# Second routed experts: a 32 bit product as three products of rounded halves

## The chip, the cores and the metric

One Trainium2 chip, one NeuronCore. The metric is the time of one execution on the device in microseconds (us); less is better. The engines named here are PE (TensorE; PEld is its weight load), DVE (VectorE), ACT (ScalarE), POOL (GpSimd) and SP (SyncE).

## The reference

Sixteen sequences of 256 rows of 128 features (4096 rows) go through four sublayers, each added to its input and normalised: attention with 16 heads of 64, routed experts (8, two for each row, F = 512), attention with 16 heads of 8, and a second block of experts. The change lies in the last one:

```python
sh = gelu(jnp.einsum('nd,sdh->snh', xf, sw1) + sb1[:, None, :])          # S = 2 shared experts, all rows
shared_out = (jnp.einsum('snh,shd->nd', sh, sw2) + sb2.sum(0)) / S
topv, topi = jax.lax.top_k(xf @ router_w + router_b, TOP_K)              # 2 of E = 8
h = gelu(jnp.einsum('nd,edh->enh', xf, w1) + b1[:, None, :])             # D = 128, H = 256
y = jnp.einsum('enh,ehd->end', h, w2) + b2[:, None, :]
moe_out = jnp.einsum('ne,end->nd', comb, y)                              # only the chosen ones count
```

## The kernel before

The program is a row of stages. `attention0_routed0` and `attention1` scatter each row, once for each of its two experts, into a table in HBM (`xs`), ordered by expert. `routed1` then takes the table in N = 39 blocks of BR = 256 rows, all of one block for one expert. `final1` gathers, weighs and normalises the results. A block ends each stage: an engine that is through with its list waits there for the others.

For block j `routed1` does this:

- SP loads the block's rows (`xrow`, 8 slots).
- PE turns them (`turn_input`, two 128x128 transposes, L1284) into XT, one PSUM bank that serves every block in turn.
- ACT copies XT to `x` (`turned`, L1354, two slots) and counts `x_done`. PE's next `turn_input` waits for that count.
- DVE copies the expert's first weights to `wu` (`weights`, L1395, four slots), works out the rows' destinations (`destinations`, L1409) and counts `w_done`.
- PE multiplies (`up`, L1266: two products of 128x128 weights with 256 columns in float32, each of which is two records in the trace).
- ACT applies gelu (`units`, L1347).
- PE multiplies with the second weights (`down`, L1276), DVE adds the bias and moves the result to `yrow` (`output`, L1401), and POOL scatters it to HBM with two indirect DMAs (L1254). `yrow` has eight slots.

Between these lie the shared experts for the last LATE = 3 groups of 512 rows, in KS = 12 steps, one for every three blocks: `shared_up` (PE, L101 to L103, three products of 512 columns), `shared_hidden` (ACT, gelu L1366 and a rounded copy L1369), `shared_low` (DVE, L1419), `shared_down` (PE, L101 to L103), and after four such steps `shared_rows` (PE, L1309) and `add_shared` (DVE, L1425). Also ACT makes two diagonals for each of the first 32 blocks (L1360). When PE is through with the last `down` it does `residual` for eight banks (L1313) and is then at the end of the stage.

The order of work on each engine is written out by hand: engines run their own lists in order, and only semaphores tie them together. The orders around the change are these loops over j:

```python
# PE                                  # ACT                             # DVE
up(j); down(j - 1)                    units(j)                          weights(j + 2); destinations(j)
turn_input(j + 2)                     shared_hidden((j - 2) / 3)        output(j - 1)
shared_up((j - 1) / 3)                turned(j + 2)                     shared_low((j - 2) / 3)
shared_down((j - 3) / 3)              diagonals(j)
```

where a shared step stands only at the j that is divisible. Elsewhere in the kernel (`attention0_routed0`, and the shared steps here) a product is already made of halves by `split_mm`: a high half is the value rounded to float32r, the low half is the rest, and three products are summed: high times high, low times high, high times low.

Of the kernel before, what the change touches and what calls it, by code (L numbers as in the profile page):

```python
# [12 lines left out]
F32 = mybir.dt.float32  # L13
F32R = mybir.dt.float32r
# [3 lines left out]
ALU = mybir.AluOpType  # L18
# [3 lines left out]
P = 128  # L22
# [1160 lines left out]
def routed1(nc, ctx, g, d):  # L1183
# [5 lines left out]

    expert, w_at, in_at = g.expert, g.w_at, g.in_at  # L1190
    xrow = sb("xrow", [P, XSLOTS, 2, XW])
    wu = sb("wu", [P, WSLOTS, F1])
    dest = sb("dest", [P, YSLOTS, 2], U32)
    x = sb("x", [P, 2, BR])
    hid = sb("hid", [P, 2, FB1, BR])
    yrow = sb("yrow", [P, YSLOTS, 2, P])
    th, pr = sb("th", [P, NTL]), sb("pr", [P, 2, NTL])
# [10 lines left out]
    def shared_step(j, at):  # L1208
        k = (j - at) // 3
        return k if (j - at) % 3 == 0 and 0 <= k < KS else None  # L1210
# [5 lines left out]
    xt_ps, x_done, up_ps, act_done, down_ps, y_done, dest_done = (sem(n) for n in (  # L1216
        "xt_ps", "x_done", "up_ps", "act_done", "down_ps", "y_done", "dest_done"))
    x_in = [sem(f"x_in{k}") for k in range(XSLOTS)]
    w_done = sem("w_done")
    y_out = [sem(f"y_out{k}") for k in range(YSLOTS)]  # L1220
    may_scatter, th_done, pr_done = sem("may_scatter"), sem("th_done"), sem("pr_done")

    def after(eng, signal, n):

        if n > 0:
            eng.wait_ge(signal, n)
# [6 lines left out]
    with nc.Block(no_gpsimd_drain=True) as block:  # L1233
# [26 lines left out]
        def _(pe):  # L1260
            def up(j):
                pe.wait_ge(x_done, j + 1)
                after(pe, act_done, j - 1)
                pe.wait_ge(w_done, j + 1)
                for f in range(FB1):
                    last = nc.tensor.matmul(H[:, j % 2, f * BR:(f + 1) * BR], wu[:, j % WSLOTS, f * P:(f + 1) * P], x[:, j % 2, :],  # L1266
                                            start=True, stop=True)
                last.then_inc(up_ps, 1)

            def down(j):  # L1270
# [69 lines left out]
        @block.scalar  # L1340
        def _(act):
            def units(j):
                w = offset(mybir.EngineType.Activation, j)
                act.wait_ge(up_ps, j + 1)
                after(act, down_ps, j - 1)
                for f in range(FB1):
                    last = nc.scalar.activation(hid[:, j % 2, f, :], H[:, j % 2, f * BR:(f + 1) * BR], ACT.Gelu,  # L1347
                                                bias=g.w1[:, bass.ds(w + (W1C + f), 1)])
                last.then_inc(act_done, 1)

            def turned(j):
                act.wait_ge(xt_ps, j + 1)
                after(act, up_ps, j - 1)
                nc.scalar.activation(x[:, j % 2, :], XT, ACT.Copy).then_inc(x_done, 1)  # L1354

            def diagonals(k):
                if k == 0:
                    act.wait_ge(pr_done, 2)
                for c in range(2):
                    nc.scalar.activation(g.diag[:, k, c, :], g.ident[:], ACT.Copy, scale=pr[:, c, k:k + 1])  # L1360

            def shared_hidden(k):
                w = k % W
                act.wait_ge(sup_ps, k + 1)
                after(act, shid_done, k - W + 1)
                nc.scalar.activation(shid[:, w, :], UP[:, k % 2, :], ACT.Gelu, bias=g.b1[:, w:w + 1]).then_inc(sact_done, 1)  # L1366
                act.wait_ge(sact_done, k + 1)
                after(act, sdown_ps, k - W + 1)
                nc.scalar.activation(shid_h[:, w, :], shid[:, w, :], ACT.Copy).then_inc(shi_done, 1)  # L1369

            def shared_mean(m):
                act.wait_ge(sdown_ps, m * W + W)
                after(act, ser_ps, m - 1)
                nc.scalar.activation(syt[:, m % 2, :], YE, ACT.Identity, bias=g.sb2m[:, 1:2], scale=1.0 / S1
                                     ).then_inc(sye_done, 1)

            nc.scalar.activation(th[:], g.gap[:], ACT.Tanh, scale=0.5).then_inc(th_done, 1)
            for j in range(-2, N):
                if 0 <= j:
                    units(j)  # L1380
                if shared_step(j, 2) is not None:
                    shared_hidden(shared_step(j, 2))
                if j + 2 < N:
                    turned(j + 2)
                if shared_group(j, 3 * W + 1) is not None:
                    shared_mean(shared_group(j, 3 * W + 1))
                if 0 <= j < NTL:
                    diagonals(j)

        @block.vector  # L1390
        def _(dve):
            def weights(j):
                w = offset(mybir.EngineType.DVE, j)
                after(dve, up_ps, j - WSLOTS + 1)
                nc.vector.tensor_copy(wu[:, j % WSLOTS, :], g.w1[:, bass.ds(w, F1)]).then_inc(w_done, 1)  # L1395

            def output(j):
                w = offset(mybir.EngineType.DVE, j)
# [27 lines left out]

            weights(0)
            weights(1)
            for j in range(N + 1):
                if j + 2 < N:  # L1430
                    weights(j + 2)
                if j < N:
                    destinations(j)
                if 0 <= j - 1:
                    output(j - 1)
                if shared_step(j, 2) is not None:
                    shared_low(shared_step(j, 2))
                if shared_group(j, 3 * W + 3) is not None:
                    add_shared(shared_group(j, 3 * W + 3))
# [1467 lines left out]
```

## Time and profile before

| what | value |
|---|---|
| three runs | 1343.93, 1343.99, 1346.85 us (median 1343.99) |
| the profiled execution | 1343.33 us |
| its span in the trace | 1341.5 us |
| mean granted clock of TensorE | 0.978 of full speed |
| busy share of the span | PE 93%, PEld 80%, DVE 73%, ACT 69%, POOL 46% |
| where `routed1` lies in the span | about 1202.5 to 1314.3 us |

The span runs from the first instruction to the last. A busy share is an average over stages with different limits; what one stage is worth is read from its own rows. Times in rows are microseconds from the span's start. A record of PE is drawn from where it starts to where its modelled end is, so records overlap, and the pace is read from start to start.

### The profile page before, as it was taken

The numbers are of one execution on the slowest core, as the hardware profiler recorded it, in microseconds if no ns is written. First come the engines' busy times: TensorE is split into PE (matmuls) and PEld (weight loads), VectorE is DVE, ScalarE is ACT, GpSimd is POOL, SyncE is SP. The second block draws the span as 40 slices with busy tenths as digits, with TensorE's granted clock in tenths as the row PEclk, the third lists the DMA queues.
The fourth block names the chain that finished last, engine by engine and source line by source line (L and its number), as shares of the span: only waits on it lengthen the run. The fifth ranks groups of instructions, "written<-read, shape, count | busy, mean of one in ns | idle before, by whom it ended". The sixth has DMA issues, their size and how long they took to land. (4 is left out here: it accounts for less than half of the span.)

```text
span 1341.5 us, 34497 instructions
## 1 busy us (share of the span) xinstructions
PE 1252.5 (93%) x10783; PEld 1070.9 (80%) x10784; DVE 976.9 (73%) x2973; ACT 921.5 (69%) x2434; POOL 618.2 (46%) x967
## 2 busy tenths in 40 slices
PE   6999999999999999999999489999999998869996
PEld 5888888888888887899999367777777776658985
DVE  6777788788878888766666488898989887363443
ACT  4777777777777776656665367878778786758863
POOL 3244444444444443453343524556556552336773
PEclk9999999999999999999999679999999999999998
DMA  8012212121202021021111522022115101113326
GB/s 267 21 53 69 67 52 75 45 85 35 91 28 92 28 88 58 15 71 57 56 54 38 190 92 77 22 89 86 43 65 174 49 17 45 60 33 106 110 73 198
DMA packets 56445, 99.82 MB, mean 74 GB/s; under 512 B 11184, under 2 KB 46384, under 8 KB 53744
## 3 DMA queue, kind: packets, MB, share of 16 engines
q1 hardware_dynamic: 45840, 78.58, 18.5%
q0 software_dynamic: 9088, 18.89, 4.2%
q10 hardware_dynamic: 1440, 1.39, 0.3%
q8 instruction: 40, 0.66, 0.2%
q14 instruction: 37, 0.30, 0.1%
HBM read 77.85 MB, written 62.06 MB: 104 GB/s over the span
## 5 line engine op out<-in xcount | busy, mean ns | idle before, releaser
L326 ACT ACTIVATE a_prob<-psum,a_nmx 128x128 f32<-128x128 f32 (+1 forms) x512 | 208.3, 425 | 82.4 <-DVE a_nmx L631 82.4
L530 POOL TENSOR_TENSOR a_prob<-a_prob,a_rl 128x128 f32<-128x128 f32 (+1 forms) x256 | 124.3, 508 | 244.1 <-DVE a_rl L635 243.5
L2373 DVE TENSOR_REDUCE a_nmx<-psum 128x2 f32<-128x512 f32 x256 | 170.1, 685 | 22.0 <-PE psum L1658 19.2
L333 ACT ACTIVATE a_probt<-psum 128x768 f32<-128x768 f32 x128 | 105.1, 821 | 70.8 <-PE psum L961 70.8
L2030 ACT ACTIVATE a_prob<-psum 128x1024 f32<-128x1024 f32 x128 | 127.3, 1024 | 7.5 <-PE psum L1688 7.3
L1658 PE MATMUL psum<-k_stk,a_q_stk 96*128 96x256 f32 x512 | 116.1, 320 | 12.8 <-DVE a_nmx L2373 8.6
L577 POOL DMA_INDIRECT yt<-a_yrow,a_dest x78 | 75.2, 964 | 101.3 <-ACT a_yrow L373 87.1
L1658 PEld LDWEIGHTS psum<-k_stk,a_q_stk 96*128 96x128 f32 x512 | 78.3, 194 | 43.3 <-issue 18.3
L326 ACT ACTIVATION_READ_ACCUMULATOR a_prob<-psum,a_nmx 128x1 f32 x512 | 107.8, 211 | 0.0
L961 PE MATMUL psum<-ident,a_prob 128*128 128x128 f32 x768 | 106.1, 274 | 1.4 <-DVE a_prob L641 1.0
L620 DVE TENSOR_TENSOR a_qkt<-psum,a_bqk 128x512 f32<-128x512 f32 x128 | 88.2, 689 | 21.7 <-PE psum L103 21.3
L773 DVE TENSOR_TENSOR a_hid<-a_wv,psum 128x512 f32<-128x512 f32 x78 | 53.6, 688 | 60.3 <-PE psum L103 44.5
L101 PE MATMUL psum<-a_x_h,a_wqk_h 128*128 128x256 f32 x312 | 94.3, 302 | 2.3 <-DVE a_wqk_l L779 2.1
L1254 POOL DMA_INDIRECT yt<-m_yrow,m_dest x78 | 75.5, 968 | 41.5 <-issue 21.2
L101 PE MATMUL psum<-a_xt_h,a_wqk_h 128*128 128x256 f32 x256 | 81.9, 320 | 8.0 <-DVE a_xt_l L616 6.9
L103 PE MATMUL psum<-a_x_l,a_wqk_h 128*128 128x256 f32 x312 | 88.1, 283 | 0.0
L102 PE MATMUL psum<-a_x_h,a_wqk_l 128*128 128x256 f32 x312 | 88.1, 282 | 0.0
L961 PEld LDWEIGHTS psum<-ident,a_prob 128*128 128x128 f32 x768 | 85.8, 141 | 2.1 <-POOL a_prob L530 1.0
L631 DVE TENSOR_REDUCE a_nmx<-psum 128x2 f32<-128x512 f32 x128 | 87.1, 680 | 0.0
L1688 PE MATMUL psum<-a_q_stk,k_stk 128*128 128x256 f32 x512 | 85.4, 290 | 0.2 <-DVE a_o L2388 0.2
L2229 POOL DMA_INDIRECT xs<-a_nrm,a_idx x60 | 61.6, 1027 | 43.3 <-DVE a_idx L2459 24.9
L2015 ACT ACTIVATE k_stk<-psum,a_in_head 96x256 fp32r<-96x256 f32 x192 | 74.5, 467 | 9.8 <-PE psum L1652 9.7
(385 smaller groups left out, 3859.6 us busy)
## 6 DMA issues: line engine op xcount, KB each, us to landing
xs<-in_fill SPq DMA_DIRECT2D x144, 264.0 KB, 4.3
a_xrow<-xs SPq DMA_DIRECT2D x39, 132.0 KB, 2.1
m_xrow<-xs SPq DMA_DIRECT2D x39, 132.0 KB, 2.2
w<-in_w SPq DMA_DIRECT2D x16, 256.0 KB, 3.5
a_yin<-yt SPq DMA_DIRECT2D x16, 256.0 KB, 2.6
f_yin<-yt SPq DMA_DIRECT2D x7, 512.0 KB, 8.2
w<-in_wr SPq DMA_DIRECT2D x2, 1284.0 KB, 7.7
xs<-in_fill_idle SPq DMA_DIRECT2D x2, 1056.0 KB, 6.6
```

The lines of the kernel that those rows point to most:

```text
L101: nc.tensor.matmul(out, wh, xh, start=start, stop=False)
L102: nc.tensor.matmul(out, wl, xh, start=False, stop=False)
L103: return nc.tensor.matmul(out, wh, xl, start=False, stop=stop)
L326: last = nc.scalar.activation(prob[:, hp % 4, h, at], S[:, 2 * (hp % 2) + h, at], ACT.Exp, bias=nmx[:, hp % 4, q, h:h + 1], accum_out=lsum ...
L333: nc.scalar.activation(probt[:, hp % 2], PT[:, :, 0:SW], ACT.Copy).then_inc(pt_done, 1)
L530: last = nc.gpsimd.tensor_tensor(prob[:, hp % 4, 0, at], prob[:, hp % 4, 0, at], rl[:, hp % 4, 0, q:q + 1].to_broadcast(prob[:, hp % 4, 0, ...
L620: nc.vector.tensor_tensor(qkt[:, hp % 2], QK.rearrange("p (j t) -> p j t", j=2), bqk[:, hp, :].unsqueeze(2).to_broadcast([P, 2, T]), ALU.a ...
L631: nc.vector.reduce_max(nmx[:, hp % 4, 1, :], two[:, :, P:SW], AX.X, negate=True).then_inc(nmx_done, 1)
L961: last = nc.tensor.transpose(PT[:, h, k * P:(k + 1) * P], prob[:, hp % 4, h, k * P:(k + 1) * P], g.ident[:])
L1658: last = nc.tensor.matmul(bank[:, q * T:(q + 1) * T], q_stk[0:KR, p, h // HG, q * P:(q + 1) * P], k_stk[p][0:KR, h, :], start=True, stop=True)
L2030: nc.scalar.activation(prob[:, k % 2, 2 * (t % 2):2 * (t % 2) + 2, :], ST[:, 2 * (t % 2):2 * (t % 2) + 2, :], ACT.Exp, scale=SCALE).then_i ...
L2373: nc.vector.reduce_max(nmx[:, :, h:h + 1], bank.rearrange("p (q k) -> p q k", q=QB), AX.X, negate=True).then_inc(mx_done, 1)
```

## The change

The two float32 products of `up` become six of halves through `split_mm`. ACT's copy of XT is now a rounding to `x_h`, DVE's copy of the weights a rounding to `wu_h`. DVE gets two new instructions for each block: `weights_low` (`wu_l`, SBUF minus SBUF, 128x256) and `input_low` (`x_l`, XT in PSUM minus `x_h`, 128x256). The counts `w_done` and `x_done` now come from these two, and new counts (`wh_done`, `xh_done`) tie them to the high halves. XT is therefore free for the next `turn_input` only when `input_low` has read it. In DVE's list both stand behind `output(j - 1)` and ahead of `shared_low`.

```diff
-    wu = sb("wu", [P, WSLOTS, F1])
+    wu_h, wu_l = sb("wu_h", [P, WSLOTS, F1], F32R), sb("wu_l", [P, WSLOTS, F1], F32R)
-    x = sb("x", [P, 2, BR])
+    x_h, x_l = sb("x_h", [P, 2, BR], F32R), sb("x_l", [P, 2, BR], F32R)
...
                 for f in range(FB1):
-                    last = nc.tensor.matmul(H[:, j % 2, f * BR:(f + 1) * BR], wu[:, j % WSLOTS, f * P:(f + 1) * P], x[:, j % 2, :],
-                                            start=True, stop=True)
+                    units = slice(f * P, (f + 1) * P)
+                    last = split_mm(nc, H[:, j % 2, f * BR:(f + 1) * BR], wu_h[:, j % WSLOTS, units], wu_l[:, j % WSLOTS, units],
+                                    x_h[:, j % 2, :], x_l[:, j % 2, :], True, True)
...
-                nc.scalar.activation(x[:, j % 2, :], XT, ACT.Copy).then_inc(x_done, 1)
+                nc.scalar.activation(x_h[:, j % 2, :], XT, ACT.Copy).then_inc(xh_done, 1)
...
-                nc.vector.tensor_copy(wu[:, j % WSLOTS, :], g.w1[:, bass.ds(w, F1)]).then_inc(w_done, 1)
+                nc.vector.tensor_copy(wu_h[:, j % WSLOTS, :], g.w1[:, bass.ds(w, F1)]).then_inc(wh_done, 1)
+
+            def weights_low(j):
+                w = offset(mybir.EngineType.DVE, j)
+                dve.wait_ge(wh_done, j + 1)
+                nc.vector.tensor_tensor(wu_l[:, j % WSLOTS, :], g.w1[:, bass.ds(w, F1)], wu_h[:, j % WSLOTS, :].bitcast(F32), ALU.subtract
+                                        ).then_inc(w_done, 1)
+
+            def input_low(j):
+                dve.wait_ge(xh_done, j + 1)
+                after(dve, up_ps, j - 1)
+                nc.vector.tensor_tensor(x_l[:, j % 2, :], XT, x_h[:, j % 2, :].bitcast(F32), ALU.subtract).then_inc(x_done, 1)
...
             weights(0)
             weights(1)
+            weights_low(0)
+            weights_low(1)
+            input_low(0)
+            input_low(1)
             for j in range(N + 1):
...
                     output(j - 1)
+                if j + 2 < N:
+                    weights_low(j + 2)
+                    input_low(j + 2)
                 if shared_step(j, 2) is not None:
                     shared_low(shared_step(j, 2))
```

## Rows read from the trace of the kernel before

**Rows 1.** The chain that ended last, in order of time: start, us, what

```profile
1315.30 6.06 DMA f_yin<-yt
...
1321.40 12.79 PE psum L2716 x112
```

**Rows 2.** Busy us of each engine in one stretch, PEclk, DMA share, GB/s

```profile
1250.00:1260.00 10.00, 10.00 (x66) 8.95 (x65) 3.94 (x13) 8.07 (x23) 7.56 (x9) 1.00 0.37 106
```

**Rows 3.** Timeline of POOL alone, 1200 to 1341: start, us, instruction, idle before

```profile
1213.37 0.95 POOL L1254 DMA_INDIRECT yt<-m_yrow,m_dest  x1 [17.88 <-DVE m_yrow L1401]
...
1216.01 0.96 POOL L1254 DMA_INDIRECT yt<-m_yrow,m_dest  x1 [0.42 <-issue]
...
1311.55 0.95 POOL L1254 DMA_INDIRECT yt<-m_yrow,m_dest  x1 [0.31 <-DMA yt<-m_yrow,m_dest]
```

**Rows 4.** Line 1233, the stage's end: ns min/median/max, first and last start

```profile
L1233 PEldq EVENT_SEMAPHORE  x2: 51/51/51, 1313.5 to 1314.3; - x2
...
L1233 POOLq COMPARE_BRANCH  x1: 38/38/38, 1314.0 to 1314.0; - x1
```

**Rows 5.** Timeline of all engines from 1305: PE's last work in the stage

```profile
1306.35 7.03 PE L1313 MATMUL psum<-x,ident 128*128 128x512 f32 x16
```

**Rows 6.** Timeline of all engines, 1250 to 1257, around one shared step

```profile
1250.50 1.03 PE L1266 MATMUL psum<-m_x,m_wu 128*128 128x256 f32 x4
...
1252.39 0.69 ACT L1366 ACTIVATE m_shid<-psum,b 128x512 f32<-128x512 f32 x1
...
1253.11 0.63 ACT L1369 ACTIVATE k_stk<-m_shid 128x512 fp32r<-128x512 f32 x1
...
1253.65 0.37 ACT L1354 ACTIVATE m_x<-psum 128x256 f32<-128x256 f32 x1
1253.78 0.69 DVE L1419 TENSOR_TENSOR k_stk<-m_shid,k_stk 128x512 fp32r<-128x512 f32 x1 [0.78 <-ACT k_stk L1369]
...
1254.52 0.51 PE L101 MATMUL psum<-k_stk,ws 128*128 128x512 f32 x1
...
1255.33 1.03 PE L1266 MATMUL psum<-m_x,m_wu 128*128 128x256 f32 x4
```

**Rows 7.** Timeline of PE alone, the rest of that period

```profile
1256.19 1.05 PE L1276 MATMUL psum<-w,m_hid 128*128 x8
...
1258.00 0.38 PE L1266 MATMUL psum<-m_x,m_wu 128*128 128x256 f32 x1
```

**Rows 8.** Timeline of all engines in the first routed experts, 560 to 566

```profile
560.85 0.36 PE L101 MATMUL psum<-a_x_h,a_wqk_h 128*128 128x256 f32 x1
...
561.04 0.28 PE L102 MATMUL psum<-a_x_h,a_wqk_l 128*128 128x256 f32 x1
...
562.24 0.28 PE L103 MATMUL psum<-a_x_l,a_wqk_h 128*128 128x256 f32 x1
...
562.78 0.39 ACT L378 ACTIVATE a_x_h<-psum 128x256 fp32r<-128x256 f32 x1 [0.34 <-PE psum L1037]
...
563.22 0.42 DVE L784 TENSOR_TENSOR a_x_l<-psum,a_x_h 128x256 fp32r<-128x256 f32 x1
...
563.55 0.21 DVE L786 SCALAR_TENSOR_TENSOR a_dest<-a_xrow,t_expert 128x2 uint32<-128x2 f32 x1
```

**Rows 9.** Timeline of DVE alone, two stretches (outputs of blocks 2 and 35)

```profile
1216.65 0.41 DVE L1395 COPY m_wu<-w 128x256 f32 x1
...
1217.12 0.42 DVE L1401 TENSOR_TENSOR m_yrow<-psum,w 128x256 f32<-128x256 f32 x1
1217.59 0.29 DVE L1395 COPY m_wu<-w 128x256 f32 x1
...
1300.27 0.42 DVE L1401 TENSOR_TENSOR m_yrow<-psum,w 128x256 f32<-128x256 f32 x1 [0.16 <-issue]
```

**Rows 10.** Timeline of all engines, 1200 to 1216: the first block's product

```profile
1206.87 1.91 PE L1266 MATMUL psum<-m_x,m_wu 128*128 128x256 f32 x4
```

**Rows 11.** Busy us and PEclk ahead of the first scatter, as in rows 2

```profile
1210.00:1212.00 2.00, 2.00 (x14) 1.82 (x12) 0.00 (x0) 1.46 (x5) 0.00 (x0) 0.72 0.60 175
```

More of the change, by code:

```diff
@@ L1218, in routed1 @@
     x_in = [sem(f"x_in{k}") for k in range(XSLOTS)]
-    w_done = sem("w_done")
+    w_done, wh_done, xh_done = sem("w_done"), sem("wh_done"), sem("xh_done")
     y_out = [sem(f"y_out{k}") for k in range(YSLOTS)]
```

## Prediction

> **What bounds the kernel now.** I read four views, from the end backwards. The chain that ended last says only that the last stage is bound by a DMA and then by PE [rows 1]; that stage starts when `routed1` ends and is not touched, so the question is when `routed1` ends. The windows come next: in the middle of the stage PE counts as busy for all of 10 us, ACT for 8.07, POOL for 7.56, DVE for 3.94 [rows 2]. That points at PE, and a faster product on PE would then pay at once.
>
> POOL's own timeline says otherwise. Its 78 scatters of one block after another start from 1213.37 to 1311.55 [rows 3], which is 98.18/77 = 1.275 us from start to start, for 0.95 us of work and about 0.3 us of issue, almost never with a wait for data. A block costs POOL 2.55 us and three blocks 7.65. POOL is the reader's first suspect: a bound that its 46% of the span hides. The stage's end confirms it. PE reaches it at 1313.5, POOL at 1314.0 [rows 4], so POOL decides, and PE with the 16 residual records behind its last `down` [rows 5] is only 0.5 us ahead.
>
> PE's pace has to be read from start to start. An `up` starts at 1250.50 and the same one of the next shared step at 1258.00 [rows 6, 7]: 7.50 us for three blocks. PE and POOL run almost level. And PE isn't simply full: in each period there is a closed loop through ACT and DVE that sets the 7.50. It reads [rows 6, 7]: `up` start to the gelu of `shared_hidden` 1.89 (1250.50 to 1252.39); to its rounded copy 0.72; to `shared_low` 0.67; to `shared_down` 0.74; to the next `up` 0.81; that `up` 0.86; then `down`, transposes and `shared_up` to the next period's `up` 1.81. The sum is 7.50. `shared_down` starts 0.05 us after `shared_low` ended (1253.78 + 0.69 = 1254.47) [rows 6], so DVE's subtraction is what PE waits for there.
>
> **PE's products.** Two float32 products take 0.86 us (1255.33 to 1256.19) [rows 6, 7]. Products of halves with the same 256 columns stand in the first routed experts: twelve in a row, the second starts 0.19 us after the first, which follows float32 work, and then ten steps take 1.20 us, 0.12 each [rows 8]. Six cost 0.72 us behind other products of halves, and 0.79 behind float32 transposes. A period has two `up` of the first kind (behind `shared_up` and `shared_down`) and one of the second: PE gives back 0.14 + 0.14 + 0.07 = 0.35 us in three blocks, 4.4 us in 38. Since POOL sets the end, by itself this would buy almost nothing.
>
> What the pages say goes one step further: the Trainium skill (FP8 and Floating Point Precision, TensorE Precision Notes) has true float32 as four passes of the array. Three passes for four would make `up` 0.645 us instead of 0.72; the loop below would come to 7.71, and the time to about 1345.4. The row at 0.12 us per product stands against it, and I stay with the row.
>
> **DVE's new work.** `input_low` has its twin in the first routed experts: it starts 0.44 us after ACT's rounding started (562.78 to 563.22) and lets the next instruction go 0.33 us later [rows 8]. `weights_low` has no twin of its size with both inputs in SBUF; between the 0.42 of that PSUM form and the 0.69 of the 512 wide `shared_low` [rows 6, 8] I take 0.42, it being half as wide. Together 0.84 us per block, 3.3 us in the 10 us window, on top of 3.94 [rows 2]: DVE goes to about 7.3 of 10 and is not full. `weights_low` is hidden: it runs behind `output`, while ACT is still on its shared work. Without this cover it would cost 0.34 to 0.42 in each shared step. The 39 copies of `weights` (0.29 each, 0.41 where one was held up [rows 9]) stay; if the rounding makes all of them 0.41, the 0.12 lies in DVE's idle time too. ACT's rounding costs what its copy cost, 0.37 against 0.39 [rows 6, 8]. SP's and POOL's lists don't change.
>
> **The new wait.** `input_low` is not hidden in a shared step. ACT does the gelu and the rounded copy of `shared_hidden` before `turned`, and DVE's list has `input_low` ahead of `shared_low`. Before, `shared_low` started 0.67 after the copy L1369. Now ACT first starts `turned` (0.54 after L1369 [rows 6]), DVE waits 0.44 for it, and `shared_low` goes 0.33 later: 1.31 in place of 0.67. Behind `shared_low` stand the next `weights`, `destinations` and `output`; PE waits with `shared_down` and all behind it, POOL for that output. `turn_input` also waits for `input_low`, but for 0.4 us that lie inside the same wait.
>
> The loop becomes (1.89 - 0.14) + 0.72 + 0.54 + 0.44 + 0.33 + 0.74 + 0.81 + 0.72 + 1.81 = 7.86 us. That is over POOL's 7.65: the loop takes over as the bound, and the products that got faster bring nothing.
>
> **The sum.** From the output of block 2 (1217.12) to that of block 35 (1300.27) there are 11 periods, 83.15 us [rows 9]: 82.5 by the loop, and 0.65 where `shared_rows` comes in and PE has no slack. With the wait there is slack, so I count 11 x 7.86 = 86.46, which is +3.3. Behind the last period's start comes one more wait, 0.64 less the 0.14 of the `up` ahead of it, and the last two `up` give back 0.14 + 0.07: +0.3. So PE reaches the end of the stage at 1313.5 + 3.6 = 1317.1. POOL: block 35's output is at 1300.27 + 3.3 + 0.5 = 1304.1, done at 1304.5, and four blocks of 2.55 take POOL to 1314.7; it was through at 1312.5 and at the end at 1314.0, so now it is there at 1316.2. PE is later. The stage ends 1317.1 - 1314.0 = 3.1 us later, and the last stage follows unchanged.
>
> The start I take at nothing, between two bounds. At the low clock (0.72 on average from 1210 to 1212, so it rises near 1211.1 [rows 11]) the first `up` took 1.91 [rows 10]; six products at twice 0.12 would take about 1.4, and the first `input_low` adds 0.44 ahead of the second `turn_input`. The ends are -0.5 and +0.5.
>
> The profiled execution took 1343.33 us, of which the span is 1341.5; plus 3.1 it would be 1346.4. The median of the runs is 1343.99, and plus 3.1 it is 1347.1, my forecast. That is 0.23%, inside the 0.3% (4.0 us: 1339.96 to 1348.02) below which a measurement of this kernel doesn't tell a change from none. Its own range is 1345.5 to 1348.7: the start's 0.5 and 0.1 us in each of the 11 periods, either way.
>
> **Rivals.** *POOL stays the bound.* If the loop grows to 7.65 or less, because the wait is shorter by 0.2 us a step than I put together from other places, POOL's 78 scatters set the end as before: 1343.7 to 1344.5. For it speaks that POOL and PE are now level, against it the closed sum of the loop, which fits the old period to 0.01. Chance 0.20.
>
> *The clock rises later.* PE now waits more in the first blocks, and before the rise it did nothing at high clock since 1206.87 [rows 10]. If the rise came later by as long as PE had worked at the low clock then, 4.2 us, it would lose half of them, 2.1 us: 1349.2, slower. Against it: PE is still busy most of that time. Chance 0.12.
>
> *Issue on DVE.* `weights_low` reads its offset from SBUF ahead of the instruction. If each new instruction kept the next waiting 0.1 us more, the loop would be 8.06 and the time 1347.1 + 2.2 = 1349.3. Chance 0.10.
>
> *POOL is slowed.* A copy of 0.41 in place of 0.29 lay beside the scatter of 1216.01 [rows 3, 9], so the two engines can meet, and here the scatter kept its 0.96. If `weights_low` lengthened every scatter by that 0.12, POOL would need 78 x 1.395 = 108.8 us from 1213.37, end at 1322.2 and be at the stage's end at 1323.7: 9.7 us slower, 1353.7. It decides from 0.04 us per scatter (3 us over 78). The Trainium skill (SBUF — State Buffer, Who interferes with whom) has a two-port copy on VectorE holding up the descriptor writing of POOL's DMAs, and a subtraction with both inputs in SBUF contending only with POOL's reads. By that rule the new subtractions would leave the scatters alone; the trace shows the meeting but not POOL's loss. Chance 0.06.
>
> *Faster by over 4 us* would need POOL's pace below 1.22 us, under every step in its timeline: 0.03.
>
> **How the numbers follow.** My forecast holds 0.49, of which 0.07 is above 1348.02. Slower is 0.07 + 0.12 + 0.10 + 0.06 = 0.35, within 0.3% 0.42 + 0.20 = 0.62, faster 0.03. The range reaches down into the case of POOL (1343.6) and up over the two cases near 1349 (1349.8); what is left out is POOL slowed, faster, and the outer parts of the others.
>
> **What would show it.** Right: `shared_low` starts about 1.3 us after L1369, PE waits for DVE ahead of `shared_down` about 0.8 us each time, the period is near 7.86, POOL waits for `output` once a period, and PE is the last to reach line 1233. Wrong: POOL without waits and a period of 7.65; or scatters above 1.275 from start to start while their outputs are long ready; or PEclk at 0.5 after 1212.

## The result and the profile after

| | before | after |
|---|---|---|
| median of the runs on the same chips | 1343.85 us (22 runs) | 1347.36 us (22 runs) |
| ratio, 95% interval | | 1.0027 [1.0021, 1.0034] |
| the profiled execution, its span | 1343.33, 1341.5 us | 1348.51, 1346.7 us |
| `routed1`, from SP's first load of rows to the stage's end | 1202.97 to 1314.35: 111.4 us | 1203.80 to 1317.29: 113.5 us |
| the last stage, from there to the end of the span | 27.15 us | 29.4 us |

The forecast was 1347.1 us. The change costs 3.5 us, and the quicker products of `up` bring nothing to the end. In the profiled pair the difference is 5.2 us: `routed1` starts 0.8 later, takes 2.1 longer, and the last stage takes 2.2 longer. The 0.8 comes from unchanged code: over all 14 profiles of this study `routed1` starts between 1202.46 and 1204.82, with the old products as with the new. The way from the first load to the output of block 2 varies too, from 13.3 to 14.8 us, with the old products (13.3 to 14.2) as with the new: the granted clock rises 6.2 us after the first load in one profile and 9.2 in another. The length of a stage in one profile is therefore good to about a microsecond. What repeats is the way from the output of block 2 to that of block 35: 83.1 and 83.2 us in the two profiles with the old products and lists (`before`, `warm_before`), 85.7 in all three of the changed ones (`after`, `after_again`, `warm_after`).

Timeline of all engines in the changed kernel, 1250 to 1260, around one shared step (as in [rows 6]); the columns are start, length, instruction and what it waited for:

```profile
1252.33 0.28 PE L101 MATMUL psum<-m_x_h,m_wu_h 128*128 128x256 f32 x1
1252.33 0.42 DVE L1401 TENSOR_TENSOR m_wu_l<-w,m_wu_h 128x256 fp32r<-128x256 f32 x1 [0.17 <-issue]
...
1253.04 1.05 PE L1277 MATMUL psum<-w,m_hid 128*128 x8
...
1254.07 0.69 ACT L1367 ACTIVATE m_shid<-psum,b 128x512 f32<-128x512 f32 x1
...
1254.79 0.63 ACT L1370 ACTIVATE k_stk<-m_shid 128x512 fp32r<-128x512 f32 x1
...
1255.33 0.36 ACT L1355 ACTIVATE m_x_h<-psum 128x256 fp32r<-128x256 f32 x1
...
1255.73 0.43 DVE L1407 TENSOR_TENSOR m_x_l<-psum,m_x_h 128x256 fp32r<-128x256 f32 x1 [0.46 <-ACT m_x_h L1355]
1256.07 0.68 DVE L1431 TENSOR_TENSOR k_stk<-m_shid,k_stk 128x512 fp32r<-128x512 f32 x1
...
1256.30 0.41 PE L1285 MATMUL psum<-ident,m_xrow 128*128 128x128 f32 x2 [0.23 <-DVE m_x_l L1407]
1256.67 0.29 DVE L1396 CAST m_wu_h<-w 128x256 fp32r x1
1256.74 1.05 POOL L1254 DMA_INDIRECT yt<-m_yrow,m_dest  x1 [0.30 <-issue]
1256.80 0.19 PEld L101 LDWEIGHTS psum<-k_stk,ws 128*128 128x128 f32 x1 [0.33 <-DVE k_stk L1431]
1256.81 0.50 PE L101 MATMUL psum<-k_stk,ws 128*128 128x512 f32 x1
...
1257.62 0.28 PE L101 MATMUL psum<-m_x_h,m_wu_h 128*128 128x256 f32 x1
...
1258.22 0.96 POOL L1254 DMA_INDIRECT yt<-m_yrow,m_dest  x1 [0.43 <-issue]
1258.32 1.05 PE L1277 MATMUL psum<-w,m_hid 128*128 x8
```

The same of PE alone, 1251 to 1262, the next period's `up`:

```profile
1260.12 0.28 PE L101 MATMUL psum<-m_x_h,m_wu_h 128*128 128x256 f32 x1
```

Read it from `up` at 1252.33, as [rows 6] were read: to the gelu 1.74, to the rounded copy 0.72, to `turned` 0.54, to `input_low` 0.40, to `shared_low` 0.34, to `shared_down` 0.74, to `up` 0.81, that `up` 0.70, and 1.80 to the next `up` at 1260.12. The sum is 7.79 us; the prediction had put 7.86 together from other places. DVE waits 0.46 for ACT's `turned`, and PE waits 0.23 ahead of the transposes and 0.33 ahead of `shared_down`.

Line 1233, the stage's end, in the changed kernel (as [rows 4]):

```profile
L1233 PEldq EVENT_SEMAPHORE  x2: 51/51/51, 1317.0 to 1317.2; - x2
...
L1233 POOLq COMPARE_BRANCH  x1: 38/38/38, 1316.2 to 1316.2; - x1
```

PE is now the last, at 1317.0, and POOL comes at 1316.2. The order has turned round.

The first and the last scatter on POOL's timeline in the changed kernel (as [rows 3]):

```profile
1213.93 1.02 POOL L1254 DMA_INDIRECT yt<-m_yrow,m_dest  x1 [17.63 <-DVE m_yrow L1413]
...
1313.77 0.96 POOL L1254 DMA_INDIRECT yt<-m_yrow,m_dest  x1 [0.30 <-DMA yt<-m_yrow,m_dest]
```

That is 99.84/77 = 1.297 us from start to start, against 1.275. Twelve times, once in a period, POOL is idle for 0.43 in place of 0.30, as at 1258.22 above: it waits for the output. The long scatters add about as much as before (1.0 us, 0.8 before).

One stretch of the stage in the changed kernel, columns as in [rows 2]:

```profile
1250.00:1260.00 10.00, 9.68 (x73) 8.83 (x73) 6.91 (x22) 7.58 (x22) 7.31 (x8) 1.00 0.37 109
```

DVE went from 3.94 to 6.91 (7.3 foreseen). PE is no longer busy all the time, which is the trace of the new wait. DVE's new instructions last 0.42 us each (35 of each kind in the middle of the stage: mean 0.425 and 0.420), as foreseen.

The chain that ended last, in the changed kernel (as [rows 1]):

```profile
1317.29 4.62 DMA f_yin<-yt
...
1321.95 17.39 PE psum L2735 x128
```

And the windows of the last stage, in the changed kernel:

```profile
1319.00:1321.00 2.00, 0.00 (x0) 0.00 (x0) 0.00 (x0) 0.00 (x0) 0.00 (x0) 1.00 0.88 271
1321.00:1323.00 2.00, 1.05 (x5) 1.06 (x6) 0.00 (x0) 0.00 (x0) 0.00 (x0) 0.52 0.70 217
1323.00:1325.00 2.00, 2.00 (x11) 2.00 (x11) 0.00 (x0) 0.00 (x0) 0.00 (x0) 0.50 1.03 341
1325.00:1327.00 2.00, 2.00 (x11) 2.00 (x11) 1.19 (x9) 0.00 (x0) 0.00 (x0) 0.50 1.09 385
1327.00:1329.00 2.00, 2.00 (x16) 2.00 (x15) 0.60 (x5) 0.00 (x0) 1.04 (x1) 0.78 1.09 386
```

Before the change, the same view has two such stretches:

```profile
1317.00:1319.00 2.00, 1.90 (x9) 1.90 (x10) 0.00 (x0) 0.00 (x0) 0.00 (x0) 0.50 0.81 244
1319.00:1321.00 2.00, 1.68 (x9) 1.49 (x8) 0.28 (x2) 0.00 (x0) 0.00 (x0) 0.66 0.94 299
```

PE waited for the first load for 5.0 us (3.7 before), and when it began, at 1321.95, the granted clock was at the lower of its two levels, 1.2 GHz (0.50): from 1321.07 to 1327.90, 6.8 us in place of 3.4. Before, that low stretch was spent on 16 products ahead of a second load, which PE had to wait for anyway (the chain of [rows 1] is a load of 6.06 us and then 112 products). After, the chain is the first load and all 128 products, many of them at half speed.

### The profile page after: what moved, and what is told of

Its sections match the earlier page's. It is cut to its first block and busy times, and to the rows that moved or that the text cites. A ratio compares the mean times of both kernels' runs of the same rounds, so it can differ in the third digit from the quotient of the medians.

```text
span 1346.7 us, 34846 instructions
## 1 busy us (share of the span) xinstructions
PE 1253.0 (93%) x10861; PEld 1072.5 (80%) x10862; DVE 1002.4 (74%) x3051; ACT 923.1 (69%) x2434; POOL 618.8 (46%) x967
## 5 line engine op out<-in xcount | busy, mean ns | idle before, releaser
L1677 PE MATMUL psum<-k_stk,a_q_stk 96*128 96x256 f32 x512 | 116.2, 320 | 12.6 <-DVE a_nmx L2392 8.4
```

Source lines behind the costliest of these rows:

```text
L1677: last = nc.tensor.matmul(bank[:, q * T:(q + 1) * T], q_stk[0:KR, p, h // HG, q * P:(q + 1) * P], k_stk[p][0:KR, h, :], start=True, stop=True)
```

## The experiments

Twelve runs, each beside runs of the kernel before on the same chip. The median of those was 1342.86 us beside `wait_only`, `no_input_low` and the two `down_later`, 1343.65 beside `reordered` and the `warm` runs, and 1344.13 beside `no_weights_low`, `no_lows`, `turned_first` and `after_again`. So compare ratios, and not medians, across the table. "Stage" is `routed1` and "last" the last stage, in the profiled execution, measured as in the first table. The two columns on POOL split its time from the first to the last scatter: idle time over the usual 0.30 ahead of a scatter, and length over the usual 0.96 of scatters that are longer.

| run | median us | ratio [95%] | stage | last | POOL idle, long |
|---|---|---|---|---|---|
| before | 1343.85 | 1 | 111.4 | 27.15 | 0.1, 0.8 |
| the change | 1347.36 | 1.0027 [1.0021, 1.0034] | 113.5 | 29.4 | 1.5, 1.0 |
| `after_again` | 1348.34 | 1.0025 [1.0015, 1.0035] | 112.9 | 28.9 | 1.5, 0.9 |
| `wait_only` | 1349.46 | 1.0047 [1.0033, 1.0060] | 117.1 | 26.3 | 5.4, 1.0 |
| `no_weights_low` | 1347.94 | 1.0035 [1.0022, 1.0048] | 113.2 | 29.3 | 1.9, 0.9 |
| `no_input_low` | 1345.74 | 1.0024 [1.0015, 1.0033] | 112.0 | 28.0 | 0, 2.0 |
| `no_lows` | 1346.99 | 1.0017 [1.0008, 1.0025] | 112.2 | 28.7 | 0, 1.8 |
| `reordered` | 1347.22 | 1.0027 [1.0018, 1.0036] | 113.0 | 27.6 | 0, 3.0 |
| `turned_first` | 1347.29 | 1.0022 [1.0013, 1.0030] | 113.1 | 28.2 | 1.5, 0.5 |
| `down_later_after` | 1349.34 | 1.0044 [1.0031, 1.0058] | 116.2 | 28.3 | 3.4, 1.2 |
| `down_later_before` | 1346.93 | 1.0026 [1.0015, 1.0036] | 113.5 | 29.5 | 3.0, 0.1 |
| `warm_before` | 1343.31 | 0.9999 [0.9990, 1.0008] | 110.5 | 26.7 | 0.1, 0.8 |
| `warm_after` | 1346.26 | 1.0024 [1.0015, 1.0033] | 113.0 | 27.2 | 1.5, 1.0 |
| `warm_reordered` | 1346.54 | 1.0022 [1.0013, 1.0032] | 113.6 | 27.05 | 0, 2.9 |

Without these two parts POOL's way from first to last scatter is a constant: 98.18 - 0.12 - 0.79 = 97.3 us before, and 97.2 to 97.5 in the change, `reordered`, `no_lows`, `no_input_low` and `wait_only`.

All versions but `warm_before` are slower than the kernel before by an interval that leaves out 1. Among themselves most can't be told apart: of the versions with the new products only `down_later_after` lies above the change by nearly a whole interval, and taking the wait away (`no_input_low`, `no_lows`, `reordered`) gives back nothing that the medians resolve. What separates them are the rows of their profiles, one execution each: these show what sets the stage's end.

**Is it the wait for `input_low`?** Three runs take the change apart. The first adds the wait and nothing else to the kernel before:

```diff
-                nc.scalar.activation(x[:, j % 2, :], XT, ACT.Copy).then_inc(x_done, 1)
+                nc.scalar.activation(x[:, j % 2, :], XT, ACT.Copy).then_inc(xh_done, 1)
...
+            def input_low(j):
+                dve.wait_ge(xh_done, j + 1)
+                after(dve, up_ps, j - 1)
+                nc.vector.tensor_tensor(x_l[:, j % 2, :], XT, x[:, j % 2, :], ALU.subtract).then_inc(x_done, 1)
```

> The kernel before with its float32 products, plus input_low on DVE in its place, whose result nobody reads, and with x_done counted by it. Theory: the loop grows by 0.64 to 8.14 us, 11 periods give 7.0 less the 0.65 of slack, plus 0.6 in the last one: 7 us, 1351. The wait costs more than the change lost, because the faster products had hidden part. Rival, that the two subtractions are hidden on DVE: 1344.

Its timeline of all engines, around a shared step:

```profile
1256.42 0.63 ACT L1369 ACTIVATE k_stk<-m_shid 128x512 fp32r<-128x512 f32 x1
1256.96 0.36 ACT L1354 ACTIVATE m_x<-psum 128x256 f32<-128x256 f32 x1
...
1257.36 0.42 DVE L1400 TENSOR_TENSOR m_x_l<-psum,m_x 128x256 fp32r<-128x256 f32 x1 [1.06 <-ACT m_x L1354]
1257.70 0.68 DVE L1424 TENSOR_TENSOR k_stk<-m_shid,k_stk 128x512 fp32r<-128x512 f32 x1
...
1258.43 0.19 PEld L101 LDWEIGHTS psum<-k_stk,ws 128*128 128x128 f32 x1 [0.33 <-DVE k_stk L1424]
```

From L1369 to `shared_low` it is 1.28 us, as in the changed kernel (1254.79 to 1256.07), against 0.67 before. With the old, slower products the period is 8.09 (from the `shared_low` at 1249.61 to that at 1257.70), 0.59 above 7.50, and the stage is 5.7 us longer: 11 x 0.59 less the 0.65 of slack. The wait does that by itself, in the median too (1.0047), and the new products then take back 3.6 us of it in the profiled stages. It is near what was expected of it (a loop of 8.14, and 7 us).

The other two leave out one of the low halves each. In `no_weights_low` the third product reads `wu_h` where `wu_l` stood, and the subtraction is gone:

```diff
-            weights_low(0)
-            weights_low(1)
...
-                    weights_low(j + 2)
```

> The changed kernel without weights_low: the second product takes wu_h in place of wu_l (the low half of the weights is left out). input_low stays where it was. Theory of the loop: weights_low was hidden, so the period stays at 7.79 us and the time at 1347, within 1 us. Rival, that the sum of DVE's new work sets the pace: half of the loss comes back, 1345.5.

The period is 7.79, the same as in the changed kernel, and so are PE's waits (0.22 and 0.34). So `weights_low` is hidden, as the prediction had it. The median, 1347.94, is where it was expected.

`no_input_low` does the same with `input_low`, and ACT's rounding counts `x_done` again:

```diff
-                nc.scalar.activation(x_h[:, j % 2, :], XT, ACT.Copy).then_inc(xh_done, 1)
+                nc.scalar.activation(x_h[:, j % 2, :], XT, ACT.Copy).then_inc(x_done, 1)
...
-                    input_low(j + 2)
```

> The changed kernel without input_low: the third product takes x_h in place of x_l (the low half of the rows is left out) and ACT counts x_done. weights_low stays. Theory: the loop is 7.50 - 0.28 = 7.22 us, under POOL's 7.65, so POOL sets the end: 1344. Rival, that weights_low, or six products in place of two, or DVE's load is the loss: 1347.

Line 1233 in `no_input_low`:

```profile
L1233 PEldq EVENT_SEMAPHORE  x2: 51/51/51, 1308.5 to 1314.5; - x2
...
L1233 POOLq COMPARE_BRANCH  x1: 38/38/38, 1314.2 to 1314.2; - x1
```

PE is through 5.7 us ahead of POOL, so the wait is gone and POOL decides again. But the kernel isn't back at 1.000, as I had expected: POOL waits for nothing and needs 1.2 us more than before, all of it in longer scatters, of up to 1.40 us. That and the 0.85 us of its last stage are not all of the 3 us that its ratio of 1.0024 stands for; the rest stays open. `no_lows` leaves out both low halves:

> The changed kernel without both subtractions: the second and third products take the high halves again (all low halves are left out), ACT and DVE's rounding count x_done and w_done. Six products remain. Theory that DVE's subtractions lengthen some of POOL's scatters (1.302 us from start to start in reordered, 1.291 in no_input_low, 1.275 before): here POOL is back at 1.275, its 78 scatters take 98.2 us from first to last start, and PE waits 5 us or more at the stage's end. Time 1343 to 1345, the last stage's low clock included. Rival, that six products or the rounding copy slow POOL: 1.29 or more, and 1345.5 or more.

There too PE is far ahead (1310.5, POOL 1316.1), the loop is 7.19, and POOL still loses 1.0 us more in long scatters than before. Its pace is 1.289 us from start to start. So the theory that DVE's new subtractions lengthen the scatters failed here: both are gone, and the scatters are still longer. What lengthens them comes below.

**Can the wait be had for nothing?** Two orders of work that keep all of it. `reordered` puts DVE's `input_low` behind `shared_low`, and PE's `shared_down` ahead of `turn_input` in the shared steps:

```diff
-                if j + 2 < N:
+                if j + 2 < N and shared_step(j, 3) is None:
...
+                    if j + 2 < N:
+                        turn_input(j + 2)
...
-                    input_low(j + 2)
                 if shared_step(j, 2) is not None:
                     shared_low(shared_step(j, 2))
+                if j + 2 < N:
+                    input_low(j + 2)
```

> The changed kernel, all its work kept, with two swaps: DVE does shared_low ahead of input_low, and PE does shared_down ahead of turn_input in a shared step. Theory of the closed loop: shared_low starts 0.67 after the rounded copy again, and what waits for input_low is now behind shared_down, so the loop is 7.50 - 2 x 0.14 = 7.2 us, under POOL's 7.65. POOL sets the stage's end as in no_input_low, PE reaches it some 5 us earlier than POOL. The last stage may then start with PE at its low clock, as there: 1345.5; without that effect 1343. Rival, that two more DVE instructions or six products cost in themselves: 1347.

PE is 4.1 us ahead of POOL (1311.7 and 1315.8), and POOL never waits. Still the time is that of the change, 1347.22, where 1343 to 1345.5 was expected: the 1.4 us of waiting that POOL no longer has came back as 2.0 us in longer scatters (pace 1.302).

`turned_first` moves ACT's `turned` ahead of `shared_hidden`:

```diff
-                if shared_step(j, 2) is not None:
-                    shared_hidden(shared_step(j, 2))
                 if j + 2 < N:
                     turned(j + 2)
+                if shared_step(j, 2) is not None:
+                    shared_hidden(shared_step(j, 2))
```

> The changed kernel, all its work kept, with ACT doing turned(j + 2) ahead of shared_hidden. DVE's wait for ACT's rounding goes, but the gelu now stands behind turned, which waits for PE's transposes: from the end of up(j) 0.89 + 0.22 + 0.31 = 1.42 to turned, 0.26 to the gelu, 0.72, 0.67, 0.74 to shared_down: 3.81 us, against 0.31 + 0.72 + 0.72 + 0.54 + 0.44 + 0.33 + 0.74 = 3.80 now. Theory of the loop: no gain, 1347 within 1 us. Rival, that the queue behind input_low on DVE is the cause by itself: it goes, and 2 us come back, 1345.

PE no longer waits for `input_low`, but it waits for `shared_low` for 5.0 us in all (12 times, up to 0.5). The loop goes through `turned` all the same, now ahead of the gelu, and the period is 7.73.

Two runs move PE's `shared_down`, and `shared_mean`, `shared_rows` and `add_shared` with it, one block later, once in the changed kernel and once in the one before:

```diff
-                if shared_step(j, 3) is not None:
-                    shared_down(shared_step(j, 3))
+                if shared_step(j, 4) is not None:
+                    shared_down(shared_step(j, 4))
```

> The changed kernel with shared_down (and the mean, rows and add behind it) one block later in the lists. Theory of the closed loop through input_low: PE no longer stands behind shared_low, a period is PE's own sum, 2 x 0.72 + 0.79 + 3 x (0.89 + 0.22) + 2 x 0.78 = 7.1 us, which is under POOL's 7.65, so POOL sets the end again: about 1344 us, level with the kernel before. Rival, that the loss comes from DVE's load on POOL or from the last stage: it stays near 1347.

> The kernel before with the same move. Theory: PE's wait for shared_low goes too, but POOL's 78 scatters set the end, so nothing changes: 1344, within 1 us; PE's outputs come earlier and wait for POOL. Rival, that PE's pace of 7.50 was the bound: PE's own sum is 3 x (0.86 + 0.89 + 0.22) + 2 x 0.78 = 7.47, which would also change little; the two differ in whether POOL waits for output, which by the theory it never does.

I had expected 1344 of the first and no change of the second, and both are slower. PE's waits in `down_later_after` over the middle of the stage (who waited for what: total, times, longest):

```profile
PE psum L1277 <- DVE m_yrow L1413: 3.5, 11, 0.8
PE psum L1285 <- DVE m_x_l L1407: 2.8, 12, 0.3
```

The wait for `shared_low` is gone and two others are there: `turn_input` waits for `input_low`, since XT is a single bank, and `down` waits for the output of the block before. The period is 7.97 in place of 7.79. So the 0.4 us of `turn_input`, which the prediction took to lie inside the wait for `shared_low`, are a wait of their own once that one is removed. The move also costs something by itself, as the kernel before shows. It puts `shared_down` right behind `shared_up` in one block, so one output in three comes late. DVE's outputs and POOL's scatter there, in `down_later_before`:

```profile
1251.04 0.42 DVE L1401 TENSOR_TENSOR m_yrow<-psum,w 128x256 f32<-128x256 f32 x1 [1.87 <-PE psum L1276]
...
1254.06 0.42 DVE L1401 TENSOR_TENSOR m_yrow<-psum,w 128x256 f32<-128x256 f32 x1 [1.61 <-PE psum L1276]
...
1255.27 0.96 POOL L1254 DMA_INDIRECT yt<-m_yrow,m_dest  x1 [0.80 <-DVE m_yrow L1401]
```

The two outputs are 3.02 us apart where POOL needs one every 2.5, and POOL waits 3.0 us in all. The theory had it that POOL never waits.

**What lengthens the scatters.** In `no_lows`, the timeline of all engines around one of them:

```profile
1251.81 0.96 POOL L1254 DMA_INDIRECT yt<-m_yrow,m_dest  x1 [0.30 <-issue]
...
1253.01 0.69 DVE L1431 TENSOR_TENSOR k_stk<-m_shid,k_stk 128x512 fp32r<-128x512 f32 x1 [0.79 <-ACT k_stk L1370]
1253.07 1.47 POOL L1254 DMA_INDIRECT yt<-m_yrow,m_dest  x1 [0.30 <-issue]
```

And in `reordered`:

```profile
1254.77 0.42 DVE L1403 TENSOR_TENSOR m_wu_l<-w,m_wu_h 128x256 fp32r<-128x256 f32 x1
1254.82 1.20 POOL L1254 DMA_INDIRECT yt<-m_yrow,m_dest  x1 [0.30 <-DVE m_yrow L1415]
```

Each time the scatter starts while DVE is already inside an instruction that reads SBUF alone, and ends 0.83 or 0.84 after that instruction has ended: 1253.70 to 1254.54 and 1255.19 to 1256.02. In the changed kernel's first fence the scatter at 1256.74 stands 0.07 inside the cast that ends at 1256.96, and ends at 1257.79. I took all 14 profiles together. `shared_low`, `weights_low` and the copy or cast of `weights` read SBUF alone. Of the scatters that start at least 0.06 us inside one of them with at least 0.17 left, all 107 end 0.82 to 0.85 after it (18, 17 and 72 for the three). Of the 46 or so that start within 0.03 of its start, inside it or just ahead, none is longer than 0.96; there the DVE instruction is up to 0.05 longer instead. `input_low`, `output` and `add_shared` read PSUM, and `destinations` is 0.21 long; of some 110 scatters that start as far inside one of these four, none is longer than 0.97. No long scatter stands outside this pattern. So DVE can hold a scatter that starts late by what is left of its instruction, less 0.13. That is read from rows, not tried: no run moved one of these instructions to free a scatter.

Between 0.03 and 0.06 both occur (the scatter at 1254.82 is 0.05 inside). This says where the gain went in `reordered`: its 13 long scatters are four that start inside `shared_low`, eight inside `weights_low` and one inside the cast, while the changed kernel has twelve short holds by the cast alone. In `no_lows` all five scatters that are longer than 1.00 are held by `shared_low`, an instruction of the kernel before: its 1.8 us need no new instruction, only that the scatters start at other moments of DVE's work.

The Trainium skill (SBUF — State Buffer, Who interferes with whom) says that a DVE instruction in a mode with two ports, which a copy can enter, and an instruction of GpSimd exclude each other: whoever is first has the shared port pair for the whole instruction. It says too that a subtraction with both inputs in SBUF contends only with an instruction of GpSimd that reads SBUF. Where the copy is first the rows agree with the first, to the 0.06 us that decides who was first. Where the scatter is first it holds the copy only in a part of its time. Of 56 copies that start 0.52 to 0.72 us into a scatter, 53 end 1.05 after the scatter's start, so that they take up to 0.53 in place of 0.29 (as the 0.41 in [rows 9]); the 187 that start earlier, or after 0.76, take 0.32 at the most. From the second the prediction concluded that the new subtractions leave the scatters alone, and that does not hold: 17 scatters were held by `weights_low` and 18 by `shared_low`. A scatter takes its row numbers from `m_dest` in SBUF, so it may be one of the instructions that read; no run here tells.

**The last stage.** In the `warm` runs PE has work for a part of its wait at the boundary: the last `residual` is written out as a product of its own, and three products of the same kind stand ahead of the first of the last stage, where PE would be idle (`warm_reordered` also does that `residual` six times more at the end of `routed1`):

```diff
+            for _ in range(2):
+                nc.tensor.matmul(g.psum[:, NG - 1, :], g.ident[:], g.x1[:, (NG - 1) * GT:NG * GT], start=True, stop=True)
+            nc.tensor.matmul(g.psum[:, NG - 1, :], g.ident[:], g.x1[:, (NG - 1) * GT:NG * GT], start=True, stop=False)
```

> The kernel before, with PE kept busy between the stages: residual of bank 7 is done twice more, to no effect on the result, and its real one stands at the head of the last stage (2.6 us of PE work in a gap of 3.7). Theory of the clock in the last stage: PE's granted clock doesn't fall there, the first group's 16 products take 1.8 us in place of 3.6; they are waited for by DVE, but the second group's data come only at 1321.4, so little is gained: 0 to 1.5 us faster, 1341.5 to 1343. Rival, that the clock there costs nothing: the same.

> The changed kernel with the same extra work on PE. In its profile the clock was low from 1321.2 to 1328.0 and the last stage took 29.4 us against 27.2. Theory: if that is part of what the change lost, it comes back: 1 to 2.5 us less than the changed kernel, about 1345. Rival, that the loss is all in the wait in the stage: 1347.

> reordered with PE kept busy to the end of the stage (bank 7's residual six times more) and into the last one, as in warm_after. Theory: no wait in the loop and no low clock: as warm_before, 1341.5 to 1343. Rival: as reordered.

The chain of `warm_after` and one of its windows:

```profile
1317.82 6.08 DMA f_yin<-yt
...
1323.94 12.79 PE psum L2735 x112
```

```profile
1321.00:1323.00 2.00, 1.69 (x15) 1.69 (x16) 0.00 (x0) 0.00 (x0) 0.00 (x0) 1.00 0.69 229
```

The clock stays at its higher level (1.00), and the chain has the form of [rows 1] again: 16 products are done ahead of the second load, and 112 behind it take 12.79 us. The last stage is 27.2 us, against 29.4 and 28.9. The first load is as late here (4.5 us from issue to landing) as in the changed kernel, so the late load by itself is not what cost the time; the low clock behind it was. In the kernel before the low clock costs nothing that can be measured: `warm_before` is at 0.9999 [0.9990, 1.0008].

The other profiles add two things. The length of the low stretch doesn't follow from that of PE's idle time: it is 6.8 us after 4.4 to 5.0 us of idle PE in four profiles (both of the changed kernel, `no_weights_low`, `down_later_after`), but 3.4 after 5.0 in `turned_first`, and 10.2 after 3.3 in `down_later_before`. And the late load costs the more, the longer PE then runs at the low clock: the last stage takes 27.2 us without a low stretch (`warm_after`), 28.2 with 3.4 us of it (`turned_first`), and 28.9 and 29.4 with 6.8 (the changed kernel). With an early load 3.4 us of it do no harm (26.3 in `wait_only`), but the 10.2 us in `down_later_before` make 29.5. What sets the length of the low stretch stays open.

In the medians little of this is seen. Those of the warm pair are 2.95 us apart (1.0024 and 0.9999), those of the two kernels of this case 3.5 (1.0027). The difference, 0.55 us, is what the low clock would cost the change in a median, by this estimate; it lies inside the intervals, so it isn't shown. With the stage's 2.1 us, some 1.4 of the 3.5 lie outside of it, part of which stands in `warm_after` too. How often the low stretch is long in runs without a profile isn't seen. The expected gain of `warm_after` (about 1345) was not clear of the noise, and `warm_reordered`, expected at 1341.5 to 1343, came to 1346.54: the two remedies don't add up to a gain.

> The changed kernel once more, for a second profile. Theory: the stage takes 113.5 us from its first load to the head of the last stage, with a period of 7.79; the last stage, whose first group runs at whichever clock PE is granted then, varies between 26.5 and 29.5 us from one execution to the next. Time 1347.

The second profile of the changed kernel has the same rows: PE last at 1317.5 and POOL at 1316.7, stage 112.9, last stage 28.9, chain of 128 products (17.35 us). So the low clock there was no accident of one execution of this kernel.

Why PE's idle time at the boundary grew can be seen in part. DMA queues and issues at the start of the last stage, of the kernel before and then of the changed one (issues: how many, KB each, median us to landing):

```profile
q1 hardware_dynamic: 1930, 1.91, 59.5%
...
f_yin<-yt SPq DMA_DIRECT2D x2, 256.0 KB, 2.9
```

```profile
q8 instruction: 1, 0.02, 0.7%
...
f_yin<-yt SPq DMA_DIRECT2D x2, 256.0 KB, 4.7
```

In the changed kernel a transfer of code (q8) runs beside the first load, in the one before there is none. Over the 14 profiles the two go together without an exception: nine have that transfer within 5 us of the first load's issue, and there the first loads take 4.0 to 4.7 us; five have none (the four with the old products, and `warm_reordered`), and there they take 2.9 to 3.1. PE's list is longer, with six products for each `up` in place of two, and that may have moved where code is loaded; this and that the code transfer is the cause of the late load are argued, not tried.

None of these versions is faster than the kernel before.

## Why the prediction was right

The number was right because the mechanism in `routed1` was, and in part by luck: a term that was too large and one that was missing nearly cancel.

**The bound before.** Right. The loop of 7.50 and POOL's 7.65 were both close to being the bound, and `no_input_low` and `no_lows` show what becomes of faster products alone: PE is 5.7 us early and POOL sets the end.

**The products.** Six products behind float32 transposes take 0.85 us up to the next `down` (1254.07 to 1254.92, some of it behind the last product; 0.79 foreseen), and behind other products of halves 0.70 (0.72 foreseen). The estimate by the Trainium skill (FP8 and Floating Point Precision, TensorE Precision Notes), 0.645 us, was too low here; the row at 0.12 us per product was the better guide.

**The wait.** Right in place and cause, and in DVE's part of it in size: 1.28 us from the rounded copy (L1370 now) to `shared_low` for 1.31 foreseen. PE's part was named too large: 0.8 us ahead of `shared_down`, where it is 0.33, with 0.23 more ahead of `turn_input`. The prediction had the 0.4 of `turn_input` inside the same wait; it is a wait beside it. The loop is 7.79 for 7.86: `input_low` came 0.04 sooner after `turned` than its twin in the first routed experts, and `up` was 0.02 shorter; the rest is rounding.

**The sum.** From the output of block 2 (1218.01) to that of block 35 (1303.72) it is 85.71 us, 2.56 more than [rows 9] give, where +3.3 was foreseen: 0.07 in each of 11 periods. The start came to +0.06 (0 foreseen), in a place that varies by a microsecond from profile to profile, and the tail behind block 35 to +0.05 (+0.3 foreseen). PE reaches line 1233 later by 2.7 from the stage's start, and with the 0.5 that it had in hand the stage is 2.1 us longer, not 3.1. The absolute times agree to 0.1 (PE at 1317.0 for 1317.1, POOL at 1316.2 for 1316.2) only because the profiled execution began the stage 0.8 late.

**The last stage.** "The last stage follows unchanged" is the step that failed. Its code is the same, but it is entered after a longer idle time of PE (a first load that takes 4.7 us in place of 2.9) and runs at the low clock for longer: +2.2 us in the profiled execution, and in the medians 0.55 by an estimate that the intervals don't resolve. The term of the stage was 1.0 too large (3.1 foreseen, 2.1 measured), this one was missing, and the two errors nearly cancel: 3.1 foreseen, 3.5 measured. That much is luck. What else makes up the 3.5 stays open.

**The rivals.** POOL did not stay the bound: the period went past 7.65, by 0.14 and not 0.21. The clock at the stage's start rose as before (at 1211.84 for 1211.12, with the stage 0.8 later), so that rival fell. Issue on DVE: the new instructions let the next go after 0.34, nothing to be seen. *POOL is slowed* was given 0.06, and as the cause of the 3.5 us it fell, since POOL had waits, its long scatters grew by only 0.2 us, and PE was last. But its mechanism is real. It isn't 0.12 us on each scatter beside `weights_low`; it is up to 0.5 on those that start inside an instruction of DVE that reads SBUF alone. It costs 1.0 us of POOL's time in the changed kernel (0.8 before), and 3.0 in `reordered`, where it decides.

## What to carry to other kernels

When two bounds are level, a faster engine brings nothing, and each wait added to the closed loop between the engines is paid once a period (here 2.6 us in 11 periods); write the loop out from start to start and put the new instruction in its place in each engine's list before counting what PE saves. An order of work that removes a wait moves everything else too, so look at what the scatters of POOL then start beside (0.8 us of long scatters here, 3.0 after the reordering). And a stage with the same code can still take another time when the stage ahead of it ends differently: look at how long PE is idle at the boundary and at the clock that it is granted behind it.

## What the runs showed of the hardware

- An indirect scatter of POOL (0.96 us) that starts at least 0.06 us inside a DVE copy, cast or subtraction with only SBUF inputs ends 0.82 to 0.85 us after that instruction: 107 of 107. One that starts first keeps its 0.96. Of the 107, 35 were held by a subtraction. A copy or cast of 0.29 that starts 0.52 to 0.72 us into a scatter ends 1.05 after the scatter's start (53 of 56).
- POOL's pace with waits and long scatters taken out is 97.3/77 = 1.263 us for a scatter of 128 rows, in kernels before and after alike. It is 0.96 of scatter and 0.30 to the next.
- At the start of the last stage the granted clock was at 1.2 GHz for 3.4 us in one kernel and 6.8 us in another after idle times of 3.7 and 5.0 us, but for 10.2 us after 3.3 in a third (`down_later_before`) and for 3.4 after 5.0 in a fourth (`turned_first`); with three products in that idle time it stayed at 2.4 GHz (`warm_before`, `warm_after`).
- The first load of a stage landed after 2.9 to 3.1 us in five profiles without, and after 4.0 to 4.7 us in nine with, one transfer of code (0.02 MB) in the same few microseconds. A kernel with longer lists can meet such a transfer in a stage that it didn't change.
